# Output projection of a cross-attention kernel: units in another order, first operands loaded under the last batch, the last text averages scaled inside the stage

## Chip, cores and metric

The kernel runs on one core of one Trainium2 chip. The metric is the device time of one execution in microseconds; the smaller, the better. All arithmetic that counts is fp32, done as products of a high part (fp32r) and a low part, three matmuls for each product.

## What is computed

Cut to what matters (B = 16 batches, S = 56 queries, DIM = 256, H = 16 heads of D = 128, a context of 1500 rows, of which the first 257 are the image part and 1243 the text part):

```python
q = rms_norm(layernorm(x) @ q_w + q_b, nq_s)                 # per head
out_txt = sdpa(q, rms_norm(txt @ k_w + k_b, nkt_s), txt @ v_w + v_b)
out_img = sdpa(q, rms_norm(img @ ki_w + ki_b, nki_s), img @ vi_w + vi_b)
x = x + (out_txt + out_img).reshape(B, S, H * D) @ o_w + o_b
x = x + ffn(layernorm(x))       # router, top 4 of 32 experts, and one shared expert
```

## The kernel before, in words

Keys and values are never built. The query of a head is multiplied into the key weights ("absorbed", 256 long), scores are taken against the raw context, and the softmax averages the raw context rows: an average is 256 long for the image and 256 long for the text, so 4 rows of 128 (`r` = 0 to 3) for each head and token. The value and output weights come after that, in the stage that this change is about.

The program is a row of blocks, each with its own instruction stream for SyncE (SP, which issues all DMAs), TensorE (PE), VectorE (DVE), ScalarE (ACT) and GpSimd (POOL). All engines meet at a block's end before any starts the next block. The blocks are `prologue`, `attend`, `outputs` and `experts`.

**attend** runs over 16 batches. One batch has 13 tiles of 128 context rows and 26 units (a tile and a half of the 896 head-and-query columns, `HALF` = 448). A tile of 256 KB is loaded at line 989 two tiles ahead. ACT takes the exponentials, DVE splits them and sums them, PE averages. A batch's averages are in `o_raw`; their softmax sums go through DRAM (stored at L1016, loaded as 112 x 8 at L1022, reciprocal on DVE at L1533, stored at L1027, loaded back over all partitions at L1033), POOL scales the averages with them (`scale_o`, L1723, two of 128 x 896 for each part), and SP stores them into `o_dram` (`store_o`, L1039: two DMAs of 448 KB, pieces of 224 bytes). All this runs inside the next batch for the text part and at the end of its own batch for the image part: `set_end` says at which tile SP does what. For the last batch no batch follows, and `tail` does the text part's steps alone: SP L1016, L1022, DVE L1533, SP L1027, L1033, POOL L1723, SP L1039, and a wait for the stores (L1144).

**outputs** (L1792 to L1954) has 32 units: head `h` and half `half` of the 896 tokens, in the order (0,0), (0,1), (1,0), (1,1) and so on. Unit `n` is:

- SP: `load_w(h)` once a head (384 KB: value weights 512 columns, output weights 256; four buffers), `load_o(n)` (128 x 4 x 448 fp32, 896 KB, from `o_dram`; four buffers);
- ACT `average(n)`: `o_high` (L1883); DVE `average(n)`: `o_low` (L1917), which sets `o_split`;
- once a head: ACT `weights` `vw_high` (L1876), DVE `weights` `ow_high` (L1913), POOL `vw_low` (L1950) and then `ow_low` (L1953), which sets `w_split`;
- PE `values(n)`: 12 matmuls of 448 columns into a bank; ACT and DVE `take(n)`: add the bias, high (L1891) and low (L1923);
- PE `project(n)`: 6 matmuls that add to `y` in four banks.

PE issues `values(0)`, `values(1)`, and then for each n `values(n + 2)`, `project(n)`. ACT and DVE prepare unit n + 2 ahead of `take(n)`. `o_high` and `o_low` have two buffers, `vw` two, `ow` three. PE waits for both weight splits of a head ahead of `values` of its first unit. At the end DVE adds `y` to `x` (L1940, two for each half), and the `experts` block begins with SP L2023 and PE L140.

Of the kernel before, what the change touches and what calls it, by code (L numbers as in the profile page):

```python
# [23 lines left out]
F32 = mybir.dt.float32  # L24
F32R = mybir.dt.float32r
ACT = mybir.ActivationFunctionType
ALU = mybir.AluOpType
# [40 lines left out]
GRAM, SC, SC_RING = 4, 5, 3  # L68

# [118 lines left out]
def build(nc, xT_in, ctx_in, lone_in, qw_in, kw_in, kwb_in, vw_in, small_in, router_in, bias_in, ffn_in, out):  # L188
    ctx = ExitStack()
    with ctx:  # L190
# [15 lines left out]
        with attn:  # L206
# [17 lines left out]

            proj = ExitStack()
            with proj:
# [10 lines left out]
                spent = attend(nc, ctx_in, lone_in, qw_in, kw_in, psum, ident, minus_half, zeros, small, key_scale, *by_head,  # L237
                               x_high, x_low, square_w, gram_high, gram_low, lin_rows, lin_pick, ones_r, u_dram,
                               beta_dram, o_dram, u_stage, u_raw, q_rms_wide, is_safe, u_stored, begun)
            outputs(nc, vw_in, psum, xT, zeros, small, v_bias, o_dram, spent)  # L240
# [567 lines left out]
def attend(nc, ctx_in, lone_in, qw_in, kw_in, psum, ident, minus_half, zeros, small, key_scale, bias_high, bias_low, x_high,  # L808
           x_low, square_w, gram_high, gram_low, lin_rows, lin_pick, ones_r, u_dram, beta_dram, o_dram, u_stage, u_raw,
           q_rms_wide, is_safe, u_stored, begun):  # L810

    ctx = ExitStack()
    with ctx:
        sb = lambda n, s, dt=F32: ctx.enter_context(nc.sbuf_tensor(n, s, dt))
# [139 lines left out]
        o_copied, o_scaled = sem("o_copied"), sem("o_scaled")  # L954
        block = ctx.enter_context(nc.Block())
# [28 lines left out]
        def _(sp):  # L984
# [114 lines left out]
            def body_of(safe):  # L1099
                def body(it, has_prev, has_next):  # L1100
# [3 lines left out]
                    for t in range(TILES):  # L1104
# [20 lines left out]
                        if has_next and t == 6:  # L1125
                            last = (2 * IMG_TILES - 1) % SC_RING
                            sp.wait_ge(seeded[last], PER_BANK[last] * it + 2 * IMG_TILES // SC_RING)
                            load_beta(it + 1, IMAGE)
                        if has_next and t == 7:
# [5 lines left out]

            def tail(it):
                store_o(it - 1, IMAGE)
                store_sums(it - 1, TEXT)
                load_sums(it - 1, TEXT)
                store_reciprocals(it - 1, TEXT)  # L1140
                load_reciprocals(it - 1, TEXT)
                store_o(it - 1, TEXT)
                for s in range(2):
                    sp.wait_ge(o_stored[s], 32 * B + CREDIT["o_stored"])  # L1144
# [291 lines left out]
        def _(dve):  # L1436
# [135 lines left out]
            def tail(it):  # L1572
                take(it - 1, UNITS - 1, False)
                for step in range(TEXT_RECIP + 1):
                    carried(it, step)
# [72 lines left out]
        def _(gp):  # L1648
# [107 lines left out]
            def tail(it):  # L1756
                for half in range(2):
                    scale_o(it - 1, TEXT, half)
# [30 lines left out]
    return spent  # L1789


def outputs(nc, vw_in, psum, xT, zeros, small, v_bias, o_dram, spent):  # L1792

    ctx = ExitStack()
    with ctx:
        sb = lambda n, s, dt=F32: ctx.enter_context(nc.sbuf_tensor(n, s, dt))
        sem = lambda n: ctx.enter_context(nc.semaphore(n))
        LOADS, RING, OW_RING, VCOLS, WCOLS = 4, 2, 3, 3 * DIM, 2 * DIM
# [565 lines left out]
```

## Time and profile before

| | before |
|---|---|
| runs | 1863.59 us median of 3 (1860.93 to 1867.96) |
| the profiled execution | 1862.32 us, of which 1860.5 us are the span from the first to the last instruction |
| granted TensorE clock, mean | 0.972 of 2.4 GHz |
| PE busy | 1723.5 us (93% of the span) |
| DVE, POOL, ACT busy | 1333.3 us (72%), 1182.0 us (64%), 983.2 us (53%) |
| DMA | 251.25 MB, 135 GB/s over the span |
| attend's last matmul ends | 1390.9 us after the span's start |
| outputs | 1409.8 to 1558.75 us, experts from there |

Times are microseconds from the start of the span; a group's mean is in nanoseconds. In a timeline row "[x <-Y]" is the time for which the engine was idle ahead of it and what ended that. SPq is SyncE issuing a DMA: the length is that of the issue, not of the transfer. A clock of 1.00 is 2.4 GHz and 0.50 is 1.2 GHz. DMA share is the mean busy share of the 16 DMA engines.

### The profile page before, as it was taken

How to read it: one execution, taken by the hardware profiler on the slowest of the kernel's cores; microseconds unless marked ns; L12 is line 12 of the kernel's file. 1: busy time of each engine (PE TensorE's matmuls, PEld its weight loads, DVE VectorE, ACT ScalarE, POOL GpSimd, SP SyncE). 2: the span in 40 equal slices, each digit the busy share in tenths (PEclk: the TensorE clock that was granted, in tenths of full speed). 3: DMA queues.
4: the chain of work that ended last, by engine and by line, in shares of the span. 5: the costliest groups of instructions: out<-in, count | busy, mean ns of one | idle time of the engine just before them, and what ended most of it. 6: DMA issues, size and time to landing. Idle time of an engine off the chain costs nothing. (4 is left out here: it accounts for less than half of the span.)

```text
span 1860.5 us, 31204 instructions
## 1 busy us (share of the span) xinstructions
PE 1723.5 (93%) x8731; PEld 1538.9 (83%) x8731; DVE 1333.3 (72%) x2561; ACT 983.2 (53%) x1657; POOL 1182.0 (64%) x1053
## 2 busy tenths in 40 slices
PE   7899899999999999999999999999983997799998
PEld 6677688989889889889889889898883886688887
DVE  4454577887887877877878878878763664677777
ACT  3455455565565655655656655665643562344343
POOL 1233578888888888888888888888752331233332
PEclk8999989999999999999999999999996998799999
DMA  3367564566466466555565665664437881233332
GB/s 113 105 236 249 182 182 105 122 126 135 116 123 133 116 120 128 132 116 123 133 124 116 127 139 121 126 134 113 86 86 242 274 266 44 76 116 115 110 117 76
DMA packets 419413, 251.25 MB, mean 135 GB/s; under 512 B 352320, under 2 KB 370880, under 8 KB 417568
## 3 DMA queue, kind: packets, MB, share of 16 engines
q1 hardware_dynamic: 419360, 250.61, 52.8%
q8 instruction: 26, 0.43, 0.1%
q14 instruction: 27, 0.22, 0.0%
HBM read 187.71 MB, written 60.10 MB: 133 GB/s over the span
## 5 line engine op out<-in xcount | busy, mean ns | idle before, releaser
L1362 ACT ACTIVATE p_high<-psum,key_rms 128x448 fp32r<-128x448 f32 x384 | 244.9, 638 | 373.2 <-PE psum L1183 373.1
L1181 PE MATMUL psum<-u_high,c_high 128*128 128x448 f32 x768 | 288.2, 375 | 37.3 <-DVE psum L1456 31.2
L1445 DVE TENSOR_TENSOR p_low<-psum,p_high 128x448 fp32r<-128x448 f32 x384 | 237.1, 617 | 90.8 <-ACT psum L1364 88.8
L1181 PE MATMUL psum<-p_high,c_high 128*128 128x448 f32 (+1 forms) x768 | 283.4, 369 | 2.9 <-DVE p_low L1445 2.9
L1182 PE MATMUL psum<-u_low,c_high 128*128 128x448 f32 x768 | 282.0, 367 | 0.0
L1183 PE MATMUL psum<-u_high,c_low 128*128 128x448 f32 x768 | 281.8, 367 | 0.0
L1183 PE MATMUL psum<-p_high,c_low 128*128 128x448 f32 (+1 forms) x768 | 280.9, 366 | 0.0
L1182 PE MATMUL psum<-p_low,c_high 128*128 128x448 f32 (+1 forms) x768 | 280.9, 366 | 0.0
L1456 DVE COPY psum<-beta_wide 128x448 f32<-128x448 f32 x416 | 259.3, 627 | 20.3 <-DMA beta_wide<-absorbed_biases 4.5
L1661 POOL TENSOR_TENSOR c_low<-stage,c_high 128x512 fp32r<-128x512 f32 x208 | 269.3, 1295 | 0.0
L1364 ACT ACTIVATE psum<-psum,key_rms 128x448 f32<-128x448 f32 x384 | 232.9, 607 | 0.0
L1655 POOL TENSOR_TENSOR key_rms<-key_ms,minus_half 128x1 f32<-128x1 f32 x209 | 119.2, 570 | 170.2 <-DVE key_ms L1470 167.8
L1181 PEld LDWEIGHTS psum<-u_high,c_high 128*128 128x128 f32 x768 | 145.2, 189 | 68.8 <-DVE psum L1456 44.1
L2068 POOL TENSOR_TENSOR scaled_gate<-gated,p_wide 128x448 f32<-128x448 f32 x64 | 83.6, 1307 | 153.9 <-ACT gated L2169 150.6
L1470 DVE CUSTOM_DVE_ANT_0 junk<-psum,c_twice 128x257 bf16<-128x257 f32 x208 | 89.0, 428 | 116.5 <-POOL c_twice L1674 93.2
L1674 POOL TENSOR_TENSOR c_twice<-stage,c_low 128x256 f32<-128x256 f32 x208 | 153.7, 739 | 16.4 <-POOL c_low L1661 2.4
L1181 PEld LDWEIGHTS psum<-p_high,c_high 128*128 128x128 f32 (+1 forms) x768 | 144.1, 188 | 15.9 <-DVE p_low L1445 7.0
L1503 DVE TENSOR_TENSOR p_sum<-psum,p_sum 128x448 f32<-128x448 f32 (+1 forms) x256 | 157.0, 613 | 0.0
L1183 PEld LDWEIGHTS psum<-u_high,c_low 128*128 128x128 f32 x768 | 145.2, 189 | 11.8
L1182 PEld LDWEIGHTS psum<-u_low,c_high 128*128 128x128 f32 x768 | 145.5, 190 | 10.9
L1183 PEld LDWEIGHTS psum<-p_high,c_low 128*128 128x128 f32 (+1 forms) x768 | 144.5, 188 | 11.9
L1182 PEld LDWEIGHTS psum<-p_low,c_high 128*128 128x128 f32 (+1 forms) x768 | 145.0, 189 | 8.2
(246 smaller groups left out, 4030.2 us busy)
## 6 DMA issues: line engine op xcount, KB each, us to landing
stage<-in_ctx SPq DMA_DIRECT2D x210, 256.0 KB, 2.8
averages<-o_raw SPq DMA_DIRECT2D x64, 448.0 KB, 5.2
o_stage<-averages SPq DMA_DIRECT2D x32, 896.0 KB, 5.5
u_raw<-absorbed_queries SPq DMA_DIRECT2D x60, 448.0 KB, 5.6
absorbed_queries<-u_stage SPq DMA_DIRECT2D x14, 1792.0 KB, 6.8
beta_wide<-absorbed_biases SPq DMA_DIRECT2D x32, 448.0 KB, 5.2
recip_wide<-reciprocals SPq DMA_DIRECT2D x32, 448.0 KB, 4.0
p_wide<-probs_by_expert SPq DMA_DIRECT2D x32, 448.0 KB, 3.5
```

The lines of the kernel that those rows point to most:

```text
L1181: nc.tensor.matmul(out, high, rhigh, start=start, stop=False, **kw)
L1182: nc.tensor.matmul(out, high, rlow, start=False, stop=False, **kw)
L1183: return nc.tensor.matmul(out, low, rhigh, start=False, stop=stop, **kw)
L1362: nc.scalar.activation(p_high[:, probs_slot(u), :], src, ACT.Exp, scale=key_rms[:, t:t + 1])
L1364: nc.scalar.activation(out, src, ACT.Exp, scale=key_rms[:, t:t + 1]).then_inc(exp_done, 1)
L1445: return nc.vector.tensor_tensor(out, a, b, ALU.subtract)
L1456: nc.vector.tensor_copy(psum[:, bank_of(u), 0:HALF], beta_wide[:, s, cols_of(half)])\
L1470: nc.vector.tensor_tensor_reduce(out=junk[:, :], in0=psum[:, GRAM, 0:DIM + 1], in1=c_twice[:, slot(t, TWICE_RING), :], scale=1.0 / INNER, ...
L1503: done = nc.vector.tensor_tensor(part if u in LAST_ADDS else total, part, total, ALU.add)
L1655: nc.gpsimd.tensor_tensor(key_rms[:, t:t + 1], key_ms[:, t:t + 1], minus_half[:, 0:1], ALU.pow)\
L1661: nc.gpsimd.tensor_tensor(c_low[:, k, :], stage[:, st, :], c_high[:, k, :].bitcast(F32), ALU.subtract)\
L1674: nc.gpsimd.tensor_tensor(c_twice[:, slot(t, TWICE_RING), 0:DIM], stage[:, st, nat], c_low[:, k, nat].bitcast(F32), ALU.add).then_inc(stag ...
```

## The change

1. `outputs` takes its units in the order (0,0) to (6,0), then (0,1), (7,0), (1,1), (8,0) up to (8,1), (15,0), and then (9,1) to (15,1). Half 0 runs seven heads ahead of half 1.
2. Its buffers are no longer its own but places in tensors of `attend`, whose memory now lives until `outputs` ends. Weights in split form have 8 buffers, raw averages 5, raw weights 4.
3. The first two raw weights and the first three raw averages are loaded in the last batch of `attend` at tile 5, the next two averages at tile 7 (`load_outputs`). Half 0 is tokens of batches 0 to 7, so it is in DRAM by then.
4. Of the last batch's text part, `attend` only stores the sums (`last_text`). `outputs` loads them; DVE takes the reciprocals behind `average(0)`; SP stores them and loads them wide, a weight load between each two; POOL scales `o_raw` behind `ow_low` of head 2; SP stores the averages ahead of the load of unit 7, which is (0,1), and waits for that store.
5. PE waits for `vw_split` ahead of `values` and for `ow_split` only ahead of `project`. The sum for half 0 is added to `x` two units after (15,0).

```diff
+OUT_LAG, EARLY_W, EARLY_O = 7, 2, 5
...
+            def load_outputs(t):
+                at = lambda n: o_dram[n, :, :, 0:HALF]
+                if t == 5:
+                    sp.wait_ge(o_stored[IMAGE], 32 * (B - 1) + CREDIT["o_stored"])
+                    sp.wait_ge(o_stored[TEXT], 32 * (B - 2) + CREDIT["o_stored"])
+                    for h in range(EARLY_W):
+                        sp.dma_start(w_raw[h], vw_in[h, :, :]).then_inc(early_loaded, 16)
+                    for n in range(3):
+                        sp.dma_start(o_slots[n], at(n)).then_inc(early_loaded, 16)
+                if t == 7:
+                    sp.wait_ge(u_split, 4 * B)
+                    sp.wait_ge(lone_summed, 2 * B)
+                    for n in range(3, EARLY_O):
+                        sp.dma_start(o_slots[n], at(n)).then_inc(early_loaded, 16)
             def tail(it):
                 store_o(it - 1, IMAGE)
-                store_sums(it - 1, TEXT)
-                load_sums(it - 1, TEXT)
-                store_reciprocals(it - 1, TEXT)
-                load_reciprocals(it - 1, TEXT)
-                store_o(it - 1, TEXT)
...
+                sp.dma_start(sums_dram[2 * it - 1, :].rearrange("(o n) -> o n", o=1), sum_row[0:1, 2:4, :]
+                             .rearrange("o a n -> o (a n)")).then_inc(last_text, 16)
+                sp.wait_ge(early_loaded, 16 * (EARLY_W + EARLY_O))
...
+        seq = [(h, 0) for h in range(OUT_LAG)]
+        for h in range(H):
+            seq.append((h, 1))
+            if h + OUT_LAG < H:
+                seq.append((h + OUT_LAG, 0))
...
+            sp.wait_ge(last_text, 16)
+            sp.dma_start(sum_cols[:, TEXT, :], sums_dram[2 * B - 1, :]...).then_inc(last_loaded, 16)
+            load_w(EARLY_W)
+            sp.wait_ge(last_recip, 1)
+            sp.dma_start(recip_dram[2 * B - 1, :]..., recip_cols[:, TEXT, :]).then_inc(last_recip_stored, 16)
+            load_w(EARLY_W + 1)
+            sp.wait_ge(last_recip_stored, 16)
+            sp.dma_start(recip_wide[:, TEXT, :], ...partition_broadcast(P)).then_inc(last_recip_loaded, 16)
+            load_w(EARLY_W + 2)
+            w_next = EARLY_W + 3
+            for n in range(EARLY_O, UNITS_O):
+                h, half = seq[n]
+                if n == place[0, 1]:
+                    sp.wait_ge(last_scaled, 2)
+                    for r in (2, 3):
+                        sp.dma_start(o_dram[:, :, r, (B - 1) * S:B * S]..., o_raw[:, r, :]...).then_inc(last_stored, 16)
+                    sp.wait_ge(last_stored, 32)
+                if half == 0:
+                    load_w(w_next) if w_next < H else None
+                    w_next += 1
+                load_o(n)
...
             def values(n):
-                if n % 2 == 0:
-                    pe.wait_ge(w_split, h + 1)
+                if half == 0:
+                    pe.wait_ge(vw_split, h + 1)
...
             def project(n):
+                if half == 0:
+                    pe.wait_ge(ow_split, h + 1)
...
@@ outputs, block.vector
+            weights(0)
+            average(0)
+            dve.wait_ge(last_loaded, 16)
+            V.reciprocal(recip_cols[:, TEXT, :], sum_cols[:, TEXT, :]).then_inc(last_recip, 1)
+            weights(1)
+            average(1)
+            for n in range(UNITS_O):
+                if n + 2 < UNITS_O:
+                    average(n + 2)
+                take(n)
+                if n + 2 < UNITS_O and seq[n + 2][1] == 0:
+                    weights(seq[n + 2][0])
+                if n == place[H - 1, 0] + 2:
+                    add(0)
+            add(1)
...
@@ outputs, block.gpsimd
             for h in range(H):
...
+                if h == 2:
+                    gp.wait_ge(last_recip_loaded, 16)
+                    for half in range(2):
+                        ...
+                        nc.gpsimd.tensor_tensor(at, at, recip_wide[:, TEXT, cols]..., ALU.mult).then_inc(last_scaled, 1)
```

## Rows read from the trace of the kernel before

**Rows 1.** Busy time by stretches; columns: stretch, length, busy (instructions) by engine, clock, DMA share, GB/s

```profile
1410.00:1420.00 10.00, 0.00 (x0) 0.00 (x0) 0.95 (x2) 2.35 (x3) 1.94 (x2) 0.50 0.92 316
...
1440.00:1460.00 20.00, 18.65 (x89) 16.66 (x90) 13.51 (x12) 11.69 (x13) 7.73 (x6) 1.00 0.84 269
```

**Rows 2.** Timeline from attend's last step to the first matmul of outputs

```profile
1391.48 0.25 SPq L1016 DMA_DIRECT2D sums<-sum_row  x1
...
1395.94 0.36 SPq L1033 DMA_DIRECT2D recip_wide<-reciprocals  x1
1399.53 4.09 POOL L1723 TENSOR_TENSOR o_raw<-o_raw,recip_wide 128x896 f32<-128x896 f32 x2 [13.65 <-DMA recip_wide<-reciprocals]
1403.66 1.61 SPq L1039 DMA_DIRECT2D averages<-o_raw  x2
1409.83 0.35 SPq L1819 DMA_DIRECT2D v_stage<-in_vw  x1
...
1421.52 0.71 PE L1837 MATMUL psum<-o_high,vw_high 128*128 128x448 f32 x1 [30.63 <-DVE o_low L1917]
```

**Rows 3.** Timeline of one pair of units in outputs, and the start of the next

```profile
1439.28 0.73 POOL L1953 TENSOR_TENSOR ow_low<-v_stage,ow_high 128x256 fp32r<-128x256 f32 x1 [4.45 <-DVE ow_high L1913]
...
1440.06 0.47 PE L1837 MATMUL psum<-o_high,vw_high 128*128 128x448 f32 x1 [0.65 <-POOL ow_low L1953]
...
1440.36 0.36 PE L1838 MATMUL psum<-o_low,vw_high 128*128 128x448 f32 x1
...
1447.25 0.37 PE L1839 MATMUL psum<-v_high,ow_low 128*128 128x448 f32 x1
...
1448.26 0.47 PE L1837 MATMUL psum<-o_high,vw_high 128*128 128x448 f32 x1 [0.64 <-POOL ow_low L1953]
```

**Rows 4.** Waits between 1409 and 1556 us: who waited for whom, us in total, times, longest

```profile
PE psum L1837 <- POOL ow_low L1953: 11.2, 15, 2.4
```

**Rows 5.** Groups of instructions between 1409 and 1556 us

```profile
L1917 DVE TENSOR_TENSOR o_low<-o_stage,o_high 128x1792 fp32r<-128x1792 f32 x32 | 65.2, 2038 | 50.1 <-ACT o_high L1883 50.1
L1883 ACT ACTIVATE o_high<-o_stage 128x1792 fp32r<-128x1792 f32 x32 | 54.4, 1701 | 55.8 <-PE psum L1839 51.2 <-DMA o_stage<-averages 4.6
...
L1950 POOL TENSOR_TENSOR vw_low<-v_stage,vw_high 128x512 fp32r<-128x512 f32 x16 | 33.6, 2098 | 31.9 <-ACT vw_high L1876 31.9
...
L1923 DVE SCALAR_TENSOR_TENSOR v_low<-psum,v_bias,v_high 128x448 fp32r<-128x448 f32 x32 | 21.7, 678 | 5.1 <-ACT v_high L1891 5.1
...
...
L1876 ACT ACTIVATE vw_high<-v_stage 128x512 fp32r<-128x512 f32 x16 | 9.9, 621 | 21.6 <-DMA v_stage<-in_vw 21.6
L1913 DVE CAST ow_high<-v_stage 128x256 fp32r<-128x256 f32 x16 | 4.5, 284 | 18.5 <-DMA v_stage<-in_vw 18.5
```

**Rows 6.** Timeline at the end of outputs and the start of experts

```profile
1557.48 1.27 DVE L1940 SCALAR_TENSOR_TENSOR xT<-psum,small,xT 128x448 f32<-128x448 f32 x2 [0.42 <-PE psum L1839]
1559.26 0.33 SPq L2023 DMA_DIRECT2D router<-in_router  x1
```

**Rows 7.** Short stretches, columns as in rows 1: the clock's fall, the first loads, the clock's rise

```profile
1392.90:1393.90 1.00, 0.00 (x0) 0.00 (x0) 0.00 (x0) 0.00 (x0) 0.00 (x0) 0.79 0.05 3
...
1422.00:1424.00 2.00, 2.00 (x7) 1.77 (x6) 1.73 (x1) 0.19 (x1) 1.73 (x1) 0.50 1.05 386
...
1427.00:1428.00 1.00, 1.00 (x5) 0.91 (x4) 0.00 (x0) 1.00 (x1) 0.00 (x0) 0.70 1.06 389
```

**Rows 8.** Loads of averages: issue to landing of all 32

```profile
DMA to landing us min/median/max: 5.1/5.5/12.5
```

**Rows 9.** Timeline of the last batch around tile 6

```profile
1338.05 0.35 SPq L989 DMA_DIRECT2D stage<-in_ctx  x1
1338.50 0.36 SPq L1022 DMA_DIRECT2D sum_cols<-sums  x1
...
1346.10 0.19 DVE L1533 RECIPROCAL recip_cols<-sum_cols 112x8 f32<-112x8 f32 x1
...
1348.16 0.63 ACT L1333 ACTIVATE c_high<-stage 128x512 fp32r<-128x512 f32 x1
```

More of the change, by code:

```diff
@@ L1756, in tail @@
             def tail(it):
-                for half in range(2):
-                    scale_o(it - 1, TEXT, half)
+                gp.wait_ge(o_scaled, 4 * it - 2 + CREDIT["o_scaled"])
             def maxima(it):
@@ L1788, in _, with outputs @@
             nc.clear_and_free_semaphores(begun)
-    return spent
-def outputs(nc, vw_in, psum, xT, zeros, small, v_bias, o_dram, spent):
+    return spent, places
+def outputs(nc, vw_in, psum, xT, zeros, small, v_bias, o_dram, spent, places, last_text):
+    (o_raw, sum_cols, recip_cols, recip_wide, recip_dram, sums_dram, w_raw, o_stage, o_high, o_low, vw_high, vw_low,
+     ow_high, ow_low, v_high, v_low) = places
     ctx = ExitStack()
     with ctx:
-        sb = lambda n, s, dt=F32: ctx.enter_context(nc.sbuf_tensor(n, s, dt))
@@ L1797, in outputs @@
         sem = lambda n: ctx.enter_context(nc.semaphore(n))
-        LOADS, RING, OW_RING, VCOLS, WCOLS = 4, 2, 3, 3 * DIM, 2 * DIM
-        UNITS_O = 2 * H
-        v_stage = sb("v_stage", [P, LOADS, VCOLS])
-        o_stage = sb("o_stage", [P, LOADS, 4, HALF])
-        o_high, o_low = sb("o_high", [P, RING, 4, HALF], F32R), sb("o_low", [P, RING, 4, HALF], F32R)
-        vw_high, vw_low = sb("vw_high", [P, RING, WCOLS], F32R), sb("vw_low", [P, RING, WCOLS], F32R)
-        ow_high, ow_low = sb("ow_high", [P, OW_RING, DIM], F32R), sb("ow_low", [P, OW_RING, DIM], F32R)
@@ L1805, in outputs @@
-        v_high, v_low = sb("v_high", [P, RING, HALF], F32R), sb("v_low", [P, RING, HALF], F32R)
-        Y, V_BANK = 0, 4
+        WCOLS, VCOLS = 2 * DIM, 3 * DIM
+        seq = [(h, 0) for h in range(OUT_LAG)]
[3 more added lines that the diff above has]
+                seq.append((h + OUT_LAG, 0))
+        place = {unit: n for n, unit in enumerate(seq)}
+        UNITS_O, LOADS, RAW, RING = len(seq), len(w_raw), len(o_stage), len(vw_high)
+        Y, V_BANK, TEXT = 0, 4, 1
@@ L1849, in values @@
                     w = slice(r * P, (r + 1) * P)
-                    last = three(psum[:, V_BANK + n % 4, 0:HALF], vw_high[:, h % RING, w], vw_low[:, h % RING, w],
-                                 o_high[:, i, r, :], o_low[:, i, r, :], r == 0, r == 3)
+                    last = three(psum[:, V_BANK + n % 4, 0:HALF], vw_high[h % RING][:, w], vw_low[h % RING][:, w],
+                                 o_high[n % 2][:, r, :], o_low[n % 2][:, r, :], r == 0, r == 3)
                 last.then_inc(v_done, 1)
             def project(n):
-                h, half, i = n // 2, n % 2, n % RING
+                h, half = seq[n]
+                if half == 0:
+                    pe.wait_ge(ow_split, h + 1)
                 pe.wait_ge(v_split, n + 1)
@@ L1898, in _ @@
             for n in range(UNITS_O):
[L1899 to L1900 removed]
                 if n + 2 < UNITS_O:
[L1902 removed]
+                    prepare(n + 2)
                 take(n)
```

165 lines of the change are left out of this document (95 added, 70 removed).

## The prediction

> **What bounds the kernel now.** I read the page first: PE is busy 93% of the span, so time can only come from stretches where PE stands still, where its clock is low, or where its matmuls can be spared. The change spares none. I then cut the span into stretches around its place. From 1410 to 1420 us PE is idle at a clock of 0.50, and in the steady part of outputs it is busy 18.65 of 20 us [rows 1]. The timeline shows what fills the hole: attend's last matmul ends 30.63 us before 1421.52, at 1390.9, and in between runs one chain of single steps, sums, reciprocals, scaling, stores, block end, first loads, first split [rows 2]. For the steady part I took one pair of units: 8.20 us from 1440.06 to 1448.26, of which the matmuls take 35 steps to 1447.25 and one more; 34 steps from 1440.36 take 6.89 us, so 0.2026 us each and 7.3 us a pair [rows 3]. The other 0.9 us are a wait: PE asks for both weight splits ahead of `values`, and `ow_low` on POOL comes last, 15 times, 11.2 us [rows 4]. Outputs as a whole: PE from 1421.5 to 1557.45 (0.42 us into DVE's wait that ends at 1557.48), so 135.9 us [rows 2, 6]; 576 matmuls x 0.2026 = 116.7, so 19.2 us are waits and low clock.
>
> **Step 1, the hole.** The chain leaves attend's end except its first step. SP issues the store of the sums from 1391.48 to 1391.73 [rows 2], and its three other waits (early loads, two older stores) are for things tens of us old. A block end costs 0.5 us (DVE done at 1558.75, SP issues at 1559.26 [rows 6]), so outputs starts at 1392.2. Weights 0 and averages 0 lie in SBUF, so ahead of the first matmul are `vw_high` 0.62, `o_high` 1.70, `o_low` 2.04 and small signals: 4.4 us [rows 5]. POOL's `vw_low`, at most 2.1, runs beside them. First matmul: 1396.6, against 1421.5.
>
> **Step 2, the clock.** It fell 2.6 us after PE's last matmul (0.79 in 1392.9 to 1393.9), and rose 6 us after PE's first (0.70 in 1427 to 1428) [rows 7]. The new gap is 5.7 us, longer than 2.6, so the clock still falls and unit 0 still starts low: 6 us at half level, 3 us lost, as before.
>
> **Step 3, the first units.** Each is followed through the waits. Unit 0 ends at 1401.2, unit 1 at 1404.8 (mostly low clock). ACT can overwrite `o_high` only when unit 0's values are done: 1401.4 + 1.70 + 2.04 gives unit 2 at 1405.3, a wait of 0.5; its values and `project(0)` are 18 x 0.2026, so PE wants unit 3 at 1409.0. DVE's weights for head 2 come behind `take(0)`: 1405.3 + 0.68 + 0.28 = 1406.3. POOL then does `ow_low(2)` 0.73 and now **the two scalings, 4.09 us [rows 2], ahead of `vw_low(3)`**, 2.10: 1413.2. This is what the move costs: PE waits 4.3 us for unit 3. A stall longer than 2.6 us can bring the clock down again [rows 7]. I take one more low spell of the same 6 us, 3 us; the bounds are 0 and 6. By the Trainium skill (TensorE: Matmul & The Clock Gate, Part 1), throttled is the default state and activity releases it; by that too the second spell is to be expected, and without it the sum is 3 us smaller.
>
> **Step 4, the chain behind the units.** SP stores the averages from 1411.2; the stores take 5.7 us (1403.66 to 0.5 ahead of 1409.83 [rows 2]): 1416.9. Only then is unit 7 loaded, 5.5 us [rows 8], and split, 3.8: 1426.3. PE wants unit 7 at about 1427.9 (units 3 to 6 and their projects, 4 x 3.65 from 1413.2), or 3 later with the clock low. So 0 to 0.1 us, with a reserve of 1.5. The reciprocals come at 1396.7 instead of 1394 and land by 1402.5, ahead of POOL's need at 1407. The wide load and the weight loads between them, and DVE's 0.20 for the reciprocals, lie in this reserve.
>
> **Step 5, the steady part.** `values` needs only `vw_low`, whose `vw_high` ACT makes a unit early, so the 0.9 us a pair go. Next in line are per unit DVE 2.04 + 0.68 + 0.28 = 3.0, ACT 1.70 + 0.62 + 0.62 = 2.9, POOL 2.8 where every unit has a new head [rows 5], all below PE's 3.65. The ring of two `o_high` closes in 0.25 + 1.70 + 2.04 + 12 x 0.2026 = 6.4 us for two units, below 7.3. DMA: a pair is 384 + 2 x 896 KB = 2.23 MB, in 7.3 us 305 GB/s; now 269 flow [rows 1], and 386 when loads are queued [rows 7]. So PE sets the pace. At the end 0.5 us wait for the last split as now; half 0's addition moves off nothing, since it was already beside PE.
>
> **Step 6, the early loads.** 2 x 384 and 3 x 896 KB = 3.54 MB go in at about 1335.1, behind the sums' store of tile 5. At 386 GB/s they take 9.2 us and end near 1346. Behind them on the same queue are the tile issued at 1338.05, needed at 1348.16, and the load of the sums at 1338.50, needed by DVE in its order at 1346.10 [rows 9]; behind DVE's wait are the seeds and splits of the scores, so PE feels it about 1 us later. Between 0 (the small ones slip through) and 4 (they land at 1348 and issue is slowed too) I take 1. The two at tile 7 have tiles behind them with over 5 us in hand.
>
> **Sum.** New outputs on PE: 1396.6 + 116.7 + 3 + (0.5 + 4.3 + 0.1 + 0.5) + 3 = 1524.7, against 1557.45: 32.7 less. With 1 for the last batch: 31.7. The profiled execution took 1862.3 (span 1860.5 and 1.8 around it), so 1830.6. It lies 1.3 below the median of the runs; I say 1831. Experts is unchanged.
>
> **Rivals.**
> - **DMA sets the pace** from unit 7 on: if 272 GB/s (2.23 MB in 8.2 us) is all that loads paced by freed buffers get, 12.5 pairs x 0.9 = 11 us come back: 1842. For it: share 0.84 already [rows 1]. Against: 386 GB/s seen, and one buffer more. 0.13.
> - **The last text's averages are late.** Loads take up to 12.5 us [rows 8]; with stores among queued loads unit 7 comes up to 7 us later, less the reserve, and the clock falls with it: 5 to 8 us, 1838. 0.12.
> - **The last batch is held up.** If the queue serves strictly in order and issue backs up, the sums' load and the tile are 4 to 6 us late, and PE with them: 1835 to 1837. The late tile would show on ACT first. 0.10. The Trainium skill (DMA: Bandwidth & Descriptors, Queues, rings and completion order) says that each DMA engine takes descriptors in ring order, which is the mechanism of this rival; no row here shows a small load behind 3.5 MB.
> - **The hole stays.** If outputs still cannot start without something of the chain, only waits of the steady part go, 10 us: 1853. Against: no wait of units 0 to 6 names it. 0.02.
> - **Slower: the clock stays low.** With stalls at units 0, 2, 3 and 7 close together the clock may not come back through outputs. At the lower level a unit costs 3.65 us more; after 9 such units, over the first spell, the 32 us are used up. All 32 would make 1831 + 110. For it: three stalls in 30 us. Against: in the steady part now, with a wait in each pair, the clock is 1.00 [rows 1, 3]. 0.02.
>
> **The numbers.** Forecast 0.61, rivals 0.39. About 0.5%, 9.3 us, is what can be told from no change: faster needs less than 1854. All cases but the last are below that, the hole's just: faster 0.95, same 0.02, slower 0.03. The range: below, no second low spell (3), no loss in the last batch (1), a shorter first spell (1 to 2): 1825. Above it takes in the late averages and the held batch whole and DMA's case to its full price: 1843. Left out are the last two and parts of two rivals' tails, with the forecast's own below 1825.
>
> **What would show it.** First matmul of outputs near 1397 and low; one PE wait of about 4 us on POOL's `vw_low` ahead of unit 3, right behind two o_raw scalings; no PE wait on `ow_low`; pairs of 7.3 us; unit 7 with next to no wait; the DVE reciprocal of the last batch after 1346 by a few us or not at all; experts starting about 33 us earlier. Wrong would be: pairs of 8 us with ACT waiting on `o_stage` loads (DMA), a wait at unit 7 (the chain), idle PE between 1345 and 1352 (early loads), or a clock of 0.50 beyond 1425.

## The result, and the profile after

| | kernel before | changed kernel |
|---|---|---|
| median of 4 runs each, same chip | 1864.76 us (1860.93 to 1867.96) | 1832.98 us (1831.81 to 1833.31) |
| ratio, 95% interval | | 0.983 (0.981 to 0.985) |
| profiled execution, its span | 1862.3, 1860.5 | 1832.7, 1830.9 |
| mean clock | 0.972 | 0.976 |

The change is worth 31.8 us by the medians, 1.7%; 31.7 us was the forecast. That the two agree to 0.1 us is luck: the forecast was worked out from the profiled execution before, and between the two profiled executions it is 29.6 us. The sum came out near by errors that cancel.

The rows below are of the changed kernel, whose line numbers differ from those before. The profile names a tile that several stages share by one of its names: `u_high` and `u_low` are the parts of the averages (`o_high`, `o_low`), `c_high`, `c_low`, `x_high`, `x_low` those of the value weights (`vw_high`, `vw_low`), `p_sum_high` and `rank_rows` those of the output weights (`ow_high`, `ow_low`), `p_high` and `p_low` those of v and of the last output weights. Timeline, from attend's last matmul to experts; columns as in [rows 2]:

```profile
1390.25 0.37 PE L1294 MATMUL psum<-x_low,ones_r 128*128 128x448 f32 x1
1396.82 0.71 PE L1904 MATMUL psum<-u_high,c_high 128*128 128x448 f32 x1 [6.21 <-DVE u_low L1989]
...
1404.84 0.44 PE L1904 MATMUL psum<-u_high,c_high 128*128 128x448 f32 x1 [1.47 <-DVE u_low L1989]
...
1405.41 2.02 DVE L1989 TENSOR_TENSOR u_low<-u_raw,u_high 128x1792 fp32r<-128x1792 f32 x1
1405.57 2.46 POOL L2031 TENSOR_TENSOR rank_rows<-beta_wide,p_sum_high 128x256 fp32r<-128x256 f32 x1 [3.81 <-DVE p_sum_high L1985]
1407.98 6.00 POOL L2038 TENSOR_TENSOR o_raw<-o_raw,recip_wide 128x896 f32<-128x896 f32 x2
...
1409.28 2.77 DVE L1989 TENSOR_TENSOR u_low<-u_raw,u_high 128x1792 fp32r<-128x1792 f32 x1 [1.07 <-ACT u_high L1953]
...
1412.57 1.56 DVE L1985 CAST p_sum_high<-u_stage 128x256 fp32r<-128x256 f32 x1
...
1413.95 1.31 POOL L2028 TENSOR_TENSOR c_low<-beta_wide,c_high 128x512 fp32r<-128x512 f32 x1
1414.01 1.72 SPq L1892 DMA_DIRECT2D averages<-o_raw  x2
1415.31 0.74 PE L1904 MATMUL psum<-u_high,c_high 128*128 128x448 f32 x1 [6.59 <-POOL c_low L2028]
...
1420.69 0.55 SPq L1871 DMA_DIRECT2D u_stage<-averages  x1
...
1427.83 1.71 ACT L1953 ACTIVATE u_high<-u_stage 128x1792 fp32r<-128x1792 f32 x1 [1.49 <-PE psum L1906]
...
1528.44 0.37 PE L1906 MATMUL psum<-p_high,p_low 128*128 128x448 f32 x1
...
1530.61 0.33 SPq L2108 DMA_DIRECT2D router<-in_router  x1
```

The hole of 30.63 us in [rows 2] is one of 6.21. Between 1396.82 and the last matmul PE stands still three more times: for unit 2, for unit 3, and 0.3 us at the end. The waits view (1385 to 1535 us; waited for, in total, times, longest) has no `ow_low` any more, where [rows 4] has 11.2 us in 15 waits:

```profile
PE psum L1904 <- DVE u_low L1989: 7.7, 2, 6.2
PE psum L1904 <- POOL c_low L2028: 6.6, 1, 6.6
...
PE psum L1904 <- DVE p_low L1995: 0.3, 1, 0.3
```

Busy time by stretches; columns: stretch, length, busy (instructions) of PE, PE's weight loads, DVE, ACT and POOL, clock, DMA share, GB/s:

```profile
1396.80:1399.80 3.00, 2.98 (x8) 2.70 (x9) 3.00 (x2) 0.07 (x1) 2.77 (x2) 0.50 0.46 139
1399.80:1402.00 2.20, 2.20 (x12) 2.00 (x12) 0.09 (x1) 1.07 (x1) 1.95 (x2) 0.99 0.87 193
...
1413.50:1420.30 6.80, 4.99 (x13) 4.46 (x14) 0.64 (x1) 0.05 (x1) 5.60 (x6) 0.50 0.66 153
...
1440.00:1460.00 20.00, 20.00 (x99) 18.16 (x98) 15.48 (x14) 13.58 (x15) 7.62 (x6) 1.00 0.99 343
```

PE is busy 20.00 of 20 us where it was 18.65 [rows 1]. The clock is at its lower level twice: for the first 3 us of PE's work in outputs and again behind the stall at unit 3.

For the early loads, SP's and DVE's timeline in the last batch, to be held against [rows 9]:

```profile
1335.68 2.06 SPq L1171 DMA_DIRECT2D u_stage<-averages  x3
1337.78 1.85 SPq L1013 DMA_DIRECT2D stage<-in_ctx  x1
1339.73 0.52 SPq L1046 DMA_DIRECT2D sum_cols<-sums  x1
...
1348.61 0.20 DVE L1574 RECIPROCAL recip_cols<-sum_cols 112x8 f32<-112x8 f32 x1 [2.73 <-DMA sum_cols<-sums]
```

A small load behind the big ones is waited for 2.73 us by DVE, and yet PE is no later: the last 1040 matmuls of attend, nearly three batches, take 205.8 us in both traces.

### The profile page after: what moved, and what is told of

Read it like the earlier page. It is cut to its first block and busy times, and to the rows that moved or that the text cites. A ratio compares the mean times of both kernels' runs of the same rounds, so it can differ in the third digit from the quotient of the medians.

```text
span 1830.9 us, 31219 instructions
## 1 busy us (share of the span) xinstructions
PE 1720.9 (94%) x8731; PEld 1539.7 (84%) x8731; DVE 1341.5 (73%) x2561; ACT 983.0 (54%) x1657; POOL 1187.9 (65%) x1053
```

## The experiments

Twelve runs on three chips, four to a chip, each beside runs of the kernel before. Executions differ outside the change too. Upstream of it, attend's last matmul starts anywhere from 1387.9 to 1396.0 us, 6 us apart even where everything ahead of it is the same code (f_after and f_halves, 1388.65 and 1394.99); downstream, from outputs' last matmul to the end is 301.6 to 305.8 us, the longest in e_no_scale. So beside each median stands **the stretch from attend's last matmul to that of outputs**, taken from the timeline of the profiled execution. It is 166.6 us before (1390.52 to 1557.08) and 138.2 in the changed kernel (1390.25 to 1528.44). It is one execution's figure, though, and not always one near the median: e_no_scale's profiled execution is the slowest of its four, f_lag5's the fastest.

| run | median us | ratio to before | stretch us | PE's waits at units 2, 3, and later ones over 0.8 |
|---|---|---|---|---|
| e_scale_before | 1833.69 | 0.983 (0.980 to 0.986) | 139.0 | 1.5, 3.2, 1.0 (unit 6), 4.5 (unit 7) |
| e_no_scale | 1829.82 | 0.980 (0.978 to 0.982) | 136.8 | 1.5, 0.7, 3.8 (unit 7) |
| e_old_wait | 1844.61 | 0.989 (0.986 to 0.991) | 150.0 | a wait in each pair |
| e_loads_late | 1835.62 | 0.985 (0.982 to 0.987) | 140.9 | 13.0 (unit 0), 1.6, 4.7 |
| f_after (unaltered) | 1830.40 | 0.982 (0.979 to 0.984) | 138.9 | 1.5, 6.6 |
| f_stores_ahead | 1826.37 | 0.980 (0.978 to 0.983) | 132.0 | 1.5, 3.1 |
| f_halves | 1829.40 | 0.981 (0.978 to 0.983) | 133.5 | 0.9, 2.7 |
| f_lag5 | 1841.49 | 0.988 (0.985 to 0.991) | 144.2 | 1.5, 6.6, 4.5 (unit in place 5) |
| g_both | 1831.03 | 0.981 (0.980 to 0.983) | 135.8 | 1.2, 1.2, 1.9 (unit 5) |
| g_after_again (unaltered) | 1832.69 | 0.982 (0.981 to 0.984) | 136.7 | 0.9, 6.6 |
| g_old_wait_again | 1843.52, one | | 149.5 | a wait in each pair |
| e_loads_tile6 | 1834.86 | 0.983 (0.982 to 0.985) | 139.1 | 1.5, 6.6 |

**e_old_wait: does the steady part owe its time to the weaker wait?**

```diff
                 if half == 0:
                     pe.wait_ge(vw_split, h + 1)
+                    pe.wait_ge(ow_split, h + 1)
```

> Edit: PE waits for ow_split ahead of values again, beside vw_split, as before the change. Theory (the looser wait gives 0.9 us a pair): in each of the 9 alternating pairs PE waits about 0.9 us for ow_low again, and in the first seven units about 1 us for each, less what hides in the stall at unit 3: 10 to 12 us more than the changed kernel, 1843 to 1845. Rival (the runs of units, not the wait, made the steady part faster; DMA or DVE sets the pace): no or little change, below 1836. Its runs of matmuls between waits also show whether the step of 0.2067 us, which held for 515 matmuls without a wait, is drawn anew after each wait: then some four fifths of the runs have 0.2027.

1844.6 us, as expected, and in the stretch 11.8 us more than the changed kernel. Timelines of PE and POOL in this run at the start of a pair, and the row of its waits from 1425 to 1540:

```profile
1441.18 0.37 PE L1906 MATMUL psum<-p_high,rank_rows 128*128 128x448 f32 x1
1442.03 0.72 POOL L2032 TENSOR_TENSOR rank_rows<-u_stage,p_sum_high 128x256 fp32r<-128x256 f32 x1 [5.05 <-DVE p_sum_high L1986]
1442.85 0.44 PE L1904 MATMUL psum<-u_high,c_high 128*128 128x448 f32 x1 [1.30 <-issue]
```

```profile
PE psum L1904 <- issue: 12.0, 10, 1.3
```

The wait is back ten times. The trace gives no releaser for it ("issue"), but PE starts 0.1 us after `ow_low` ends (1442.75), a longer wait of this run at unit 2 (4.7 us) names `ow_low`, and nothing else was changed. So the cause of the wait in Step 5 is shown. Its size is not the old one: the last eight take 1.30 us each, where a pair had 0.65 before, and 2.6 us are saved at units 2 to 4, where part of the stall now lies at unit 2. The total of 11.8 us says what the weaker wait is worth in the new order of units; it doesn't confirm 0.9 us a pair.

**e_scale_before: is it the scalings that hold unit 3?** The order of GpSimd's instructions:

```diff
-vw_low(0) ow_low(0) vw_low(1) ow_low(1) vw_low(2) ow_low(2) scale scale vw_low(3) ow_low(3)
+vw_low(0) ow_low(0) vw_low(1) ow_low(1) vw_low(2) scale scale vw_low(3) ow_low(2) ow_low(3)
```

> Edit: the two scalings of the last text averages stand behind vw_low of head 2 (in the 3.8 us in which POOL waited for DVE's ow_high), and vw_low of head 3 stands ahead of ow_low of head 2. Theory (the scalings' place costs PE a stall and a second low spell of the clock): reciprocals land at about 1402.3, scalings 1402.3 to 1406.6, vw_low(3) to 1408.7, PE wants it at 1408.6; the stall of 6.6 us falls below 1 us, the second low spell (3 us lost) goes, unit 7 is loaded 7 us earlier and still comes in time: about 9.5 us less than the changed kernel, 1823.5. Rival (the chain of the last text averages, not the order on POOL, sets the pace of the first units): the stall moves to unit 7, PE waits there for o_low, and under 4 us are won, 1829 or more.

Timelines of POOL, SP and PE:

```profile
1402.21 5.21 POOL L2041 TENSOR_TENSOR o_raw<-o_raw,recip_wide 128x896 f32<-128x896 f32 x2 [1.88 <-DMA recip_wide<-reciprocals]
...
1410.49 0.47 PE L1904 MATMUL psum<-u_high,c_high 128*128 128x448 f32 x1 [3.16 <-POOL c_low L2028]
1411.25 0.34 SPq L1865 DMA_DIRECT2D beta_wide<-in_vw  x1
1412.25 7.43 SPq L1892 DMA_DIRECT2D averages<-o_raw  x2
1423.07 0.55 SPq L1871 DMA_DIRECT2D u_stage<-averages  x1
...
1432.21 0.47 PE L1904 MATMUL psum<-u_high,c_high 128*128 128x448 f32 x1 [4.54 <-DVE u_low L1989]
```

The wait at unit 3 fell from 6.6 to 3.2 us, not below 1, and 4.5 us came at unit 7, with the second low spell of the clock behind it (matmuls 0.37 us apart to 1436.1). The stretch is 2.3 us longer than that of g_after_again, whose long run of matmuls had the same step (below). It is the rival's outcome. The scaled averages were ready at 1407.4, but the stores went out at 1412.25: in SP's program they stand behind the weight load of unit 6, which waits for a buffer that `ow_low(2)` frees, and that now came later. Then the two took 7.4 us to issue behind those loads, and each 9.7 on average from its issue to its landing instead of 4.9. So a move on GpSimd was paid for in SP's queue.

**e_no_scale: what are the scalings worth in all?** They are left out, so the last batch's text averages stay unscaled. SP's timeline stands behind the expectation.

```diff
-                    for half in range(2):
-                        ...
-                        nc.gpsimd.tensor_tensor(at, at, recip_wide[...], ALU.mult).then_inc(last_scaled, 1)
+                    gp.sem_inc(last_scaled, 2)
```

> Edit: POOL leaves out the two scalings (the last batch's text averages stay unscaled), all else is in place. Theory: POOL reaches vw_low(3) at about 1409.5, so PE waits about 1 to 2 us for unit 3 instead of 6.6, no second low spell of the clock, about 8 us less than the changed kernel: 1825. It bounds what the scalings cost where they stand. Rival: the stall at unit 3 has another cause (DVE's late ow_high of head 2, at 1405.5, or slow DMA): at least 4 us of it stay and the clock falls again, 1830 or more.

```profile
1410.85 7.48 SPq L1892 DMA_DIRECT2D averages<-o_raw  x2
1421.74 0.55 SPq L1871 DMA_DIRECT2D u_stage<-averages  x1
```

Unit 3 waits 0.7 us, so the scalings are what held it. But the stretch is only 1.4 us shorter than the changed kernel's: the stores again stand behind the loads of unit 6, and unit 7 waits 3.8 us. Without a remedy on SP most of what is won at unit 3 is lost at unit 7 in this execution. By the medians it is more, 1829.8 us or 0.980 of before against 0.983 (on different chips), but not the 8 us that I expected.

**f_stores_ahead: the remedy on SP.** The order of e_scale_before, and:

```diff
-                if n == place[0, 1]:
+                if n == place[6, 0]:
                     sp.wait_ge(last_scaled, 2)
                     for r in (2, 3):
                         ...
+                if n == place[0, 1]:
                     sp.wait_ge(last_stored, 32)
```

> Scalings straight behind the third weight split, as in e_scale_before, and the two stores of the scaled averages on SP ahead of the loads of the seventh head instead of behind them; the wait for their landing stays before unit 7's load. Theory (in e_scale_before the stall at unit 7 came because the stores stood on SP behind a weight load that waits for GpSimd's second output-weight split): the stores issue at about 1408 instead of 1412.3 and take about 2 us, unit 7's load issues at about 1413 to 1415 instead of 1423, the wait of 4.9 us at unit 7 is gone, and unit 3 keeps its 3 to 3.5 us: 1828.5 us (1827 to 1831), 4.5 below e_scale_before. Rival (the chain of landings, not SP's order, is what is late: the stores' packets wait behind the seven loads in the queues): unit 7's wait stays above 2 us, and the time within 1.5 us of e_scale_before's 1833.7.

```profile
1402.69 6.01 POOL L2042 TENSOR_TENSOR o_raw<-o_raw,recip_wide 128x896 f32<-128x896 f32 x2 [1.28 <-DMA recip_wide<-reciprocals]
...
1408.72 1.39 SPq L1892 DMA_DIRECT2D averages<-o_raw  x2
...
1411.76 0.47 PE L1905 MATMUL psum<-u_high,c_high 128*128 128x448 f32 x1 [3.10 <-POOL c_low L2029]
1412.97 2.33 SPq L1871 DMA_DIRECT2D u_stage<-averages  x2
...
1424.14 0.47 PE L1905 MATMUL psum<-u_high,x_high 128*128 128x448 f32 x1 [0.18 <-POOL x_low L2029]
```

The time is even below the expected 1827 to 1831. The stores go out at 1408.7 in 1.39 us, no wait at unit 7, a stretch of 132.0 us, and no second fall of the clock behind unit 3. It is the shortest stretch of all, 4.7 us below g_after_again, which drew the same step (below), and 6.2 below the changed kernel's first profile. The median is 1826.4 against 1830.4 of f_after on the same chip (five runs each, 1825.8 to 1830.5 and 1829.1 to 1832.5): 4 us, although the two intervals of the ratio to before overlap.

**f_halves: one scaling less in front of unit 3.**

```diff
-                if h == 2:
+                if h in (2, 4):
                     gp.wait_ge(last_recip_loaded, 16)
-                    for half in range(2):
-                        cols = slice(half * HALF, (half + 1) * HALF)
+                    cols = slice((h - 2) // 2 * HALF, h // 2 * HALF)
```

SP stores each half by itself, the first ahead of the load of unit (0,1), the second ahead of that of (3,1).

> The scaling for the first eight heads stays where the changed kernel has it, that for the last eight heads goes two heads later; each half is stored by itself, the second before head 3's second unit is loaded. Theory (unit 3 waits for the two scalings that stand ahead of its weight split on GpSimd, 6.6 us in the changed kernel): one scaling of 2.1 to 3.9 us goes from in front of it, unit 3's wait falls to 2.5 to 4.5 us, unit 7's load goes out some 2 to 3 us earlier too, and the time falls by 2 to 4 us: 1830 us (1829 to 1832). Rival (what stretches the scaling is that DVE works beside it, and unit 3 waits for its averages' low part on DVE anyway): the wait stays above 5.5 us and the time within 1 us of the changed kernel's.

```profile
1411.78 3.88 POOL L2040 TENSOR_TENSOR o_raw<-o_raw,recip_wide 128x896 f32<-128x896 f32 x1
...
1416.98 0.47 PE L1907 MATMUL psum<-u_high,c_high 128*128 128x448 f32 x1 [2.74 <-POOL c_low L2031]
```

The wait is 2.7 us, as expected, and the stretch 133.5, 3.2 below g_after_again with the same step. In the time only 1.0 us shows against f_after; this profiled execution ended attend 6.3 us later than f_after's.

**g_both: do the two remedies add?** f_stores_ahead, with the second scaling behind `ow_low(4)` and its stores ahead of (3,1).

> f_stores_ahead and f_halves together: the scaling for heads 0 to 7 straight behind the third weight split with its stores ahead of the seventh head's loads, the scaling for heads 8 to 15 behind the fifth head's output-weight split with its stores ahead of head 3's second unit. Theory (the two remedies act on the same piece of GpSimd's order, so they add only in part): unit 3's wait falls from the 3.5 us of f_stores_ahead to 0.5 to 1.5, no wait of over 1 us comes at unit 7 or at head 8's second unit, outputs take 124 to 125.5 us from first to last matmul against 126.0: 1824.5 us (1823 to 1827), 1.5 to 2.5 below f_stores_ahead. Rival (behind the first units DMA sets the pace, as its share of 1.05 from 1424 on suggests, and whatever is won at unit 3 is waited for again at 1425 to 1436): new waits on DVE's averages or GpSimd's weights of 1.5 us or more together in that stretch, and a time within 1 us of f_stores_ahead's 1826.4.

```profile
1411.87 0.44 PE L1908 MATMUL psum<-u_high,c_high 128*128 128x448 f32 x1 [1.22 <-DVE u_low L1993]
...
1417.04 3.90 POOL L2044 TENSOR_TENSOR o_raw<-o_raw,recip_wide 128x896 f32<-128x896 f32 x1
1420.89 1.32 POOL L2032 TENSOR_TENSOR x_low<-u_stage,x_high 128x512 fp32r<-128x512 f32 x1
...
1422.27 0.47 PE L1908 MATMUL psum<-u_high,x_high 128*128 128x448 f32 x1 [1.85 <-POOL x_low L2032]
```

They don't, and the time of 1831.0 us is 4 above the expected range. Unit 3's wait is down to 1.2, but I had not counted what the second scaling stands in front of: the split for unit 5, which PE now waits for, 1.85 us. Together the waits are as long as in f_stores_ahead. Of the 3.8 us that the stretch is longer, 1.9 are the slower of two steps (476 matmuls, below), which isn't the edit's; the rest is the clock, granted 0.74 from 1424 to 1430 behind that wait, against 1.00 in f_stores_ahead, and low for 5.4 us instead of 3.5 at the start of outputs. The spell at the start is the execution's; whether the second fall is the edit's, one profile can't say.

**f_lag5: what do seven heads buy?**

```diff
-OUT_LAG, EARLY_W, EARLY_O = 7, 2, 5
+OUT_LAG, EARLY_W, EARLY_O = 5, 2, 5
```

> The first-half units run five heads ahead instead of seven, so the first unit that needs the last stores stands in place 5 rather than 7. Theory (the chain scalings, stores, load, splits ends at about 1430, and in the changed kernel PE comes to place 7 just then, with no reserve): PE comes to place 5 about 7.3 us earlier, at 1423, and waits there for 6 to 8 us; a clock spell behind it can add up to 3: 1841 us (1839 to 1844), with no other wait changed. Rival (there is slack in the chain, the load could land earlier since its buffer is free): the wait at place 5 is under 4 us, 1837 us or less.

```profile
1418.97 0.56 SPq L1871 DMA_DIRECT2D u_stage<-averages  x1
...
1424.18 1.70 ACT L1953 ACTIVATE u_high<-u_stage 128x1792 fp32r<-128x1792 f32 x1 [16.14 <-DMA u_stage<-averages]
...
1427.99 0.47 PE L1904 MATMUL psum<-u_high,c_high 128*128 128x448 f32 x1 [4.51 <-DVE u_low L1989]
```

The time is the forecast's (1841.5), the wait is not: 4.5 us instead of 6 to 8 (the stretch grew by 6.0, the rest being the clock, which fell again behind this wait). This trace doesn't explain the time: its execution took 1836.2 us, the other three 1841.3 to 1844.0 at a mean clock of 0.973 to 0.975 against 0.978. Of the 11 us between the medians of f_lag5 and f_after some 6 are seen in the trace, and that the forecast of the time came true is in part luck. I had assumed no reserve at place 7, but there is one: in the changed kernel the load issued at 1420.69 lands 5.6 us later, at 1426.3, and ACT asks for it at 1427.83 and names PE as what it waited for. Lag seven is covered by 1.5 us; a unit is 3.7 us, so lag six would wait about 2 (an estimate).

**e_loads_late: what do the early loads buy?** No load is made under the last batch; they open outputs instead.

```diff
-                    for h in range(EARLY_W):
-                        sp.dma_start(w_raw[h], vw_in[h, :, :]).then_inc(early_loaded, 16)
-                    for n in range(3):
-                        sp.dma_start(o_slots[n], at(n)).then_inc(early_loaded, 16)
...
+            sp.dma_start(w_raw[0], vw_in[0, :, :]).then_inc(first_w_loaded[0], 16)
+            first_o(0)
+            sp.dma_start(w_raw[1], vw_in[1, :, :]).then_inc(first_w_loaded[1], 16)
+            first_o(1)
```

The loads of units 2 to 4 go between the steps of the sums' chain.

> Edit: nothing is loaded under the last batch; the two weights and five averages are loaded at the start of outputs, in the order w0, o0, w1, o1, then between the steps of the last text's chain. Theory (the early loads give what stands between the block's start and the first split): first averages land at about 1398 to 1399.6 instead of lying there, first matmul at 1402 to 1403.5 instead of 1396.8, the chain behind is as much later: 6 to 9 us more than the changed kernel, 1839 to 1842. Rival (the hole closed by moving the chain alone; the loads would hide behind other first work): below 1836. A third outcome: DMA has then 5.4 MB more to move in outputs and sets the pace in the steady part, 1845 or more.

```profile
1403.48 0.71 PE L1911 MATMUL psum<-u_high,c_high 128*128 128x448 f32 x1 [13.03 <-DVE u_low L2002]
...
1420.27 0.72 PE L1911 MATMUL psum<-u_high,c_high 128*128 128x448 f32 x1 [4.69 <-POOL c_low L2041]
```

The first matmul comes 6.8 us later after attend, as expected, but the time is 1835.6, in the range that the rival had, and the stretch is only 4.2 us longer than in g_after_again, which drew the same step. 1.9 us come back at unit 3, where PE waits 4.7 instead of 6.6. Another 1.5 us are the clock's, low for 3.1 us at the start of outputs here and for 6.1 in g_after_again, and so not the edit's. So the early loads are worth 4 to 6 us by the traces while unit 3 waits for GpSimd (3 by the medians, on different chips), and not the whole of what they take from the first gap.

**e_loads_tile6: does DVE's wait for the late sums cost anything?**

```diff
-                if t == 5:
+                if t == 6:
                     sp.wait_ge(o_stored[IMAGE], 32 * (B - 1) + CREDIT["o_stored"])
```

> The five early loads of the last batch's sixth tile go one tile later, behind the text sums' load instead of in front of it. Theory (those loads make the sums' load land 2.7 us late for DVE, but DVE and TensorE have that much in hand): the wait of DVE for the sums, 2.7 us in the changed kernel, is gone or under 0.5, TensorE's waits in the last batch stay as they are, the first unit starts at the same distance of 6.6 us behind attend's last matmul, and the time is the changed kernel's within 1 us. Rival (the sums' delay reaches the end of the batch): attend ends 1 us or more earlier and the time is 1 to 2.7 us below. Rival on the other side (the loads now land too late for the first units): a gap of over 7.5 us ahead of the first unit, and 1 us or more slower.

The reciprocal runs without a wait, but PE now waits elsewhere in the last batch (DVE's row, then PE's waits from 1300 to 1397 us):

```profile
1349.00 0.19 DVE L1574 RECIPROCAL recip_cols<-sum_cols 112x8 f32<-112x8 f32 x1
```

```profile
PE psum L1222 <- DVE p_low L1486: 2.0, 2, 1.3
```

The last 1040 matmuls of attend take 208.5 us here. In the profiles that load at tile 5 they take 205.8 to 207.0, and five of these eleven have such a wait, of 0.2 to 0.8 us; before and e_loads_late, without early loads, have none and take 205.8. So the early loads do reach PE in some executions, by up to 1.2 us. The later place looks worse (2.7 us in its one profile; 1834.9 against 1832.7 us in g_after_again, with ranges that overlap), and it wins nothing. None of my theories had this: I had looked only at the load that was late, not at what the burst would push next.

**f_after, g_after_again and g_old_wait_again: what belongs to the execution?** All unaltered.

> The changed kernel itself, unaltered, beside the three runs that follow. Its first profile and the first four experiments leave one thing unnamed: whether the start-to-start time of unwaited 448-column matmuls (0.2067 us in the 515 of the first profile, 0.2027 in others) belongs to the kernel or to the execution. Theory (drawn anew at each wait, not the kernel's): the stretches before and after each wait fall on either value again, not necessarily the same ones as in the first profile; the PE end of the outputs moves by up to 2.1 us with it. Rival (set by the addresses or by the order of the instructions): the same stretches show the same values as in the first profile. Time 1833 us (1831 to 1836) in either case; waits at unit 2 of 1.5 us and at unit 3 of 6.6 us again.

> The changed kernel unaltered a third time, beside the other three. Both its profiles so far gave 0.2067 us as the step of the long run of matmuls behind unit 3. Theory (the step is drawn anew in each execution at each wait): there is an even chance that this profile shows 0.2027 there, and the outputs then take 2.1 us less from first to last matmul. Rival (the step is fixed by the kernel): 0.2067 a third time, and the values of the two stretches before it, 0.2063 and 0.2027 in the first profile, the same too. Time 1830 to 1834 us.

> e_old_wait unaltered: twelve stretches of 35 or more matmuls, each behind a wait, gave steps of 0.2025, .2066, .2066, .2067, .2065, .2027, .2025, .2065, .2025 and .2067 us from 1426 on. Theory (drawn anew in each execution): the order of the two values differs in at least two places out of ten (by chance five). Rival (fixed by the kernel): the same order in all ten. Time 1841 to 1848 us.

Same stretch of time, same busy time of PE, first in the first profile of the changed kernel, then in g_after_again (columns: stretch, length, PE busy, clock, DMA share, GB/s):

```profile
1440.05:1528.40 88.35, 88.08 (x426) 1.00 0.68 226
```

```profile
1440.05:1528.40 88.35, 88.06 (x435) 1.00 0.69 226
```

The clock at the start of outputs in g_after_again, from 3 to 6 us after PE's restart at 1399.15 (columns: stretch, length, PE busy, clock, DMA share, GB/s):

```profile
1402.10:1405.10 3.00, 3.00 (x10) 0.50 0.84 191
```

In the first profile the clock was back after 3.1 us; here it is low to 1405.2, for 6.1 us, and in f_after for 4.2. Behind the stall at unit 3 the three have 5.0, 3.9 and 5.7 us. The program is the same: the length of a low spell, too, belongs to the execution.

With one and the same program PE starts nine matmuls more in 88.35 us at the same granted clock. From one start to the next it is 0.2067 us in the first (and in f_after), 0.2027 in the other. The ten runs of matmuls between waits from 1426 on have, in e_old_wait, steps of .2025, .2066, .2066, .2067, .2065, .2027, .2025, .2065, .2025, .2067 us, and in g_old_wait_again .2027, .2065, .2028, .2066, .2027, .2028, .2027, .2027, .2065, .2027 (each the time from a run's second start to its last, over the number of steps between). Five of ten differ, as many as by chance; so it is not fixed by the kernel. (f_after alone, with 0.2027 behind unit 2 and 0.2067 behind unit 3 as in the first profile, would have spoken for the rival.) My guess of four fifths at 0.2027 was wrong: four of ten in the first, seven in the second. As a rule the step changes only where PE has waited and holds to the next wait, over 515 matmuls in the longest case. Twice it changed inside a run: in f_stores_ahead at 1420.2 us and in e_scale_before at 1419.1, at an interruption of less than 0.1 us, which the waits view doesn't list.

## Why the prediction was right, and where it was not

PE's last matmul of outputs ends at 1528.8; the forecast was 1524.7. Of the two parts of the gain the hole gave 24.4 us (24.9 forecast), but the rest of outputs only 4.0 (7.8 forecast), and experts began 28.7 us earlier instead of 33. The total is right within 2 us because 4.1 us too little on PE in outputs stand against 1 us for the last batch that was not paid and 0.9 us by which what follows outputs was shorter in this execution (302.5 us after the last matmul's start, 303.4 before).

- **Step 1, the hole: right.** First matmul at 1396.82 against 1396.6; 24.4 us come from here (30.63 less 6.21). The chain of sums and reciprocals went on beside the first units.
- **Step 2, the clock: right in kind; its length is no constant.** It fell in the gap. In the profiled execution it did not stay low for 6 us after PE's restart but for 3.0 (eight matmuls in 3.00 us at 0.50, then 0.99); in the other two profiles of the same kernel it was 4.2 and 6.1. The old trace showed the rise only once, and I took that single interval for a constant. The 2.6 us of Step 3 are no limit either: behind waits of 3.1 and 3.2 us at unit 3 (f_stores_ahead, e_scale_before) the clock stayed at 1.00, and behind 2.7 (f_halves) and 1.9 (g_both, unit 5) it fell to 0.50.
- **Step 3, unit 2: start right, wait low.** It starts at 1404.84 (forecast 1405.3); since the clock rose earlier, PE was there earlier and waited 1.5 instead of 0.5.
- **Step 3, unit 3: the mechanism right, the term mis-sized.** PE waited for `vw_low(3)` behind two scalings, 6.6 us instead of 4.3, and e_no_scale shows that they are the cause. The term that failed is "4.09 us", with the 0.73 ahead of it. That row [rows 2] was taken while DVE stood still; here the two took 6.00 with DVE at work beside them, `ow_low(2)` took 2.46 instead of 0.73, and DVE's own operations were longer too (`o_low` 2.77 for 2.03, a cast 1.56 for 0.28). The rows above show why: the engine that begins second finishes as if it had started when the first was done. DVE's `o_low` runs from 1405.41 to 1407.43; `ow_low(2)`, begun at 1405.57, ends at 1408.03, 0.6 us after it (0.73 alone). The first scaling ends and the second begins at 1410.1; the next `o_low`, begun at 1409.28, ends at 1412.05, 1.9 us after the first scaling (2.03 alone), and the second scaling at 1413.98, 1.9 us after that `o_low` (2.05 alone). Two such waits for DVE, which add 1.7 and 1.9 us to the old rows, are the whole excess. Two errors the other way hid 1.5 us of it: POOL began 0.7 us earlier than forecast, and `vw_low(3)` took 1.31, not 2.10, for the mean of [rows 5] has such waits in it already. The second low spell came; its 13 matmuls cost 2.5 us of the 3 forecast. The Trainium skill (TensorE: Matmul & The Clock Gate, Part 1) has throttled as the default state, by which it was to be expected; the trace agrees.
- **Step 4, the chain behind the units: right.** Store to load 6.7 us (forecast 5.7), no wait at unit 7, and a reserve of 1.5 us as forecast, part of it lent by the long stall at unit 3. e_scale_before and e_no_scale show what the forecast did not see: the stores are safe only while SP comes to them before the loads of unit 6 fill its queue. That is the rival "late averages" in other clothes: it decides as soon as unit 3's stall is mended.
- **Step 5, the steady part: right.** No wait from 1420 to 1526, and a pair takes 7.44 us (36 x 0.2067; 7.3 forecast). DMA's share was 0.99 and 343 GB/s around 1450 without being waited for, so the rival of 1842 is out: what buffers allow was more than 272 GB/s. New was 2.1 us for a slower step (515 matmuls x 0.0041).
- **Step 6, the early loads: cost 0 here, up to 1.2 in other executions; 1 was taken.** The sums' load, issued at 1339.73 behind the burst, took 8.9 us to land (2.3 before) and kept DVE until 1348.61, but PE had that much in hand. The Trainium skill's rule of ring order (DMA: Bandwidth & Descriptors, Queues, rings and completion order) agrees with the late load; what failed of that rival is the step from the load to PE.

Added up for outputs on PE, each stall counted from start to start, which makes it 0.1 to 0.2 us longer than the idle time in the rows: 128.1 forecast + 2.4 (unit 3) + 1.1 (unit 2) - 2.0 (clock) + 2.2 (step) + 0.1 (the small rest) = 131.9; measured 132.0.

## What to carry to other kernels

Price an operation from a row in which its neighbours are as busy as they will be. GpSimd's work and VectorE's work with two operands in SBUF went one after the other here, so the price is the time alone plus what is left of the other engine's operation at that moment, and a mean from the table of groups is neither. Before moving work on one engine, read what stands behind it in every in-order queue that is released by it: mending the stall at unit 3 paid most when SP's stores moved as well (f_stores_ahead, 4 us below the changed kernel, the version to keep). When versions differ by a few us, compare the stretch that the edit touches, not one execution's total, which here spreads by 6 us from code that is the same, and take more than one profile of it: the step and the length of a low clock spell move even the stretch by 2 us.

## What was new of the hardware

- Back-to-back matmuls of 448 columns at the full granted clock have two start-to-start times, 0.2027 and 0.2067 us, 2% apart. One of them holds, with two exceptions, from one wait of PE to the next, and identical programs draw differently. A kernel that never waits stakes its whole stretch on one draw, 2.1 us for 515 matmuls. What selects it stays open.
- An identical `ow_low` on GpSimd took 0.73 or 2.4 to 2.5 us and one scaling 2.2 or 3.9 us in the same execution. The long ones are those that begin while a subtraction of VectorE with both operands in SBUF is running, and they last as much longer as that still runs. It holds the other way as well: in f_stores_ahead `o_low` takes 3.95 us beside GpSimd's work, 2.03 alone. VectorE's `v_low`, which reads PSUM, took 0.67 to 0.69 us whatever ran beside it. No run was made for this; it is read from starts and ends.
- At the start of outputs the clock was back at 1.00 after 3.1, 4.2 and 6.1 us of PE's work in three profiles of one program.
- Two stores of 448 KB took 1.4 us to issue and on average 4.6 each to land when SP reached them first (f_stores_ahead), and 7.4 and 9.7 us behind the two loads of unit 6, 1.28 MB (e_scale_before).
